# Message passing, last layer, steps 2 to 4: gathered rows go through PSUM before VectorE multiplies them

## The reference, cut to what matters

```
w = _kernel_net(edge_attr, ...).reshape(-1, 16, 16)      # one 16x16 matrix per edge
for i in range(DEPTH):                                   # DEPTH = 4
    msg = einsum('ei,eio->eo', nodes[src], w)            # gather a row, multiply by its edge's matrix
    agg = segment_sum(msg, dst, num_segments=n) * inv_deg
    nodes = gelu(agg + nodes @ root_W[i] + root_b[i])
```

## Time and profile before

| | us |
|---|---|
| median of 3 runs without the profiler | 26865.84 |
| lowest and highest of them | 26846.94, 26884.09 |
| span of the profiled execution, first to last instruction | 31834.1 |

### The profile page before, as it was taken

How to read it: one execution, slowest core, us unless ns; L and a number is a source line. 1 busy time by engine, 2 the same in 40 slices (tenths; PEclk the granted TensorE clock), 3 DMA queues, 4 the chain that set the end, 5 groups by cost and what they waited for, 6 DMA issues and landing times. The chain is left out here.

```text
span 31834.1 us, 357740 instructions
## 1 busy us (share of the span) xinstructions
PE 21003.5 (66%) x95045; PEld 10976.5 (34%) x95045; DVE 19470.8 (61%) x31805; ACT 12595.6 (40%) x14673; POOL 20017.5 (63%) x18077
## 2 busy tenths in 40 slices
PE   4666649999867777756666666566655656465654
PEld 2333326666533333323333333222222222222222
DVE  4444448888756666645555555566665766566665
ACT  4555511111134444431111111455555655455554
POOL 4666657777734444445555555677776777766666
PEclk8777769999877777777777777777777777777777
DMA  1111125555412222212222222444444544444443
GB/s 38 34 33 34 34 59 93 92 92 93 89 42 50 50 49 49 49 44 86 84 86 84 85 84 82 120 138 146 143 127 130 147 140 145 113 136 136 140 135 106
DMA packets 2202951, 2877.61 MB, mean 90 GB/s; under 512 B 962293, under 2 KB 1687075, under 8 KB 2175143
## 3 DMA queue, kind: packets, MB, share of 16 engines
q1 hardware_dynamic: 1369250, 2680.20, 26.7%
q0 software_dynamic: 804512, 169.87, 8.0%
q10 hardware_dynamic: 29088, 26.49, 0.2%
HBM read 2203.20 MB, written 671.60 MB: 90 GB/s over the span
## 5 line engine op out<-in xcount | busy, mean ns | idle before, releaser
L575 POOL DMA_INDIRECT got<-table,idx x15352 | 16035.5, 1045 | 10224.3 <-issue 4522.0
L777 PE MATMUL in_place<-place_hot,tparts 128*128 128x512 bf16 x37600 | 10862.7, 441 | 5734.9 <-issue 2698.7
L777 PEld LDWEIGHTS in_place<-place_hot,tparts 128*128 128x128 bf16 x37600 | 4005.5, 111 | 11806.1 <-issue 7382.3
L940 ACT ACTIVATE near<-place_b,far_lanes 128x512 bf16<-128x512 f16 x9180 | 5713.3, 707 | 61.9 <-DMA place_b<-place_row 61.4
L1078 DVE TENSOR_REDUCE msg<-prod 128x64 f32<-128x1024 f32 x4040 | 4904.5, 1214 | 103.3
L945 ACT ACTIVATE place_hot<-near,one 128x4608 bf16<-128x4608 bf16 x1020 | 4218.3, 4136 | 1004.0 <-remote 810.9
L930 ACT ACTIVATE outb<-run 128x256 f32<-128x256 f32 (+1 forms) x1010 | 739.3, 732 | 8309.1 <-DVEq L1115 6614.4
L1492 POOL DMA_INDIRECT added<-rows,add_idx x2020 | 3318.9, 1643 | 962.2 <-issue 866.7
L1070 DVE TENSOR_TENSOR prod<-w_in,got 128x1024 f32<-128x1024 f32 x2424 | 2909.9, 1220 | 303.7 <-DMA got<-table,idx 176.5
L1535 PE MATMUL acc<-hot,spread 128*128 128x392 bf16 x14544 | 2849.5, 353 | 0.0
L1063 DVE TENSOR_TENSOR wcopy<-wmat,b 128x1024 f32<-128x1024 f32 x808 | 988.3, 1223 | 2445.7 <-remote 2050.1
(11 more groups left out here) (253 smaller groups left out, 18740.6 us busy)
## 6 DMA issues: line engine op xcount, KB each, us to landing
w_in<-kept SPq DMA_DIRECT2D x2424, 512.0 KB
kept<-wcopy SPq DMA_DIRECT2D x808, 512.0 KB
got<-table,idx POOLq DMA_INDIRECT x15352
attr<-in_edge_attr SPq DMA_DIRECT2D x202, 1024.0 KB
place_b<-place_row SPq DMA_DIRECT2D x1020, 128.0 KB
range_b<-range_row SPq DMA_DIRECT2D x1015, 128.0 KB
sums<-outb SPq DMA_DIRECT2D x1010, 128.0 KB
rows<-in_src_row SPq DMA_DIRECT2D x202, 640.0 KB
```

The source lines that it names most:

```text
L575: pool.indirect_dma_start(out=dst[:, j * width:(j + 1) * width], out_offset=None, in_=table, in_offset=bass.IndirectOffsetOnAxis(ap=idx[:, ...
L777: mm = pe.matmul(in_place[b][:, h, :], tparts[:, s, t, :], place_hot[:, b, t, h * XC:(h + 1) * XC], start=(t == 0 and s == 0), stop=(t == ...
L940: act.activation(near[:, t, :], place_b[:, b, :], ACT.Abs, bias=SB["far_lanes"][:, t:t + 1]).then_inc(S["near_made"], 1)
```

## The change

In kind "kernel_kept" alone:

- ScalarE gets a step `rows_over(k)`: it waits for chunk k's 12 gathers, for VectorE to be done with chunk k-2 (`rows_read`), and copies the 12 places' rows (192 float32 per partition) from `got` in SBUF into `rows_p[k % 2]`, one PSUM bank each. It stands between `hot_rows` and `turn_out`, one chunk ahead.
- VectorE waits for that copy (`rows_made`) instead of the gathers. Its first three products read the rows from `rows_p`; the fourth reads TensorE's rows straight from `in_row`. The copy L1019 is gone. `fetched` is raised at the end of the chunk instead of before the last product, together with `rows_read`. `got_used` is not raised any more.
- GpSimd reuses a ring buffer once ScalarE has copied from it.

For the other kinds only the way ScalarE's loop is written out changes (four chunks to a loop instead of two, in the same order).

```
+            rows_p = [ps(f"rows_p{k}", [P, 512])[:, 0:J0 * W] for k in range(HALVES)]
...
+                        if kind == "kernel_kept":
+                            pool.wait_ge(S["rows_made"], k - RING + 1)
+                        else:
+                            pool.wait_ge(got_used[r], q)
...
+                def rows_over(k, b, r, q, first):
+                    act.wait_ge(got_in[r], (q + 1) * (16 * J0))
+                    if not first:
+                        act.wait_ge(S["rows_read"], k - 1)
+                    act.activation(rows_p[b], got[:, r, 0:J0 * W], ACT.Copy).then_inc(S["rows_made"], 1)
...
+                def chunk(k, r, q, at):
+                    i, b = q * (RING // HALVES) + r // HALVES, r % HALVES
+                    if at is None or at + 1 < CHUNKS:
+                        spread_mask(k + 1, 1 - b, at == 0)
+                    hot_rows(k + 2, b, i + 1)
+                    if kind == "kernel_kept" and (at is None or at + 1 < CHUNKS):
+                        rows_over(k + 1, 1 - b, (r + 1) % RING, q + (r + 1) // RING, at == 0)
+                    turn_out(k, b, i, at is not None and at < HALVES)
...
-                        dve.wait_ge(got_in[r], (q + 1) * (16 * J0))
+                        if kind == "kernel_kept":
+                            dve.wait_ge(S["rows_made"], k + 1)
+                        else:
+                            dve.wait_ge(got_in[r], (q + 1) * (16 * J0))
...
+                                if g < GROUPS - 1:
+                                    rows_g = rows_p[b].rearrange("p (j f) -> p j f", f=W)[:, g * G:(g + 1) * G, :]
+                                else:
+                                    dve.wait_ge(S["in_row_made"], k + 1)
+                                    rows_g = in_row[b].rearrange("p (j f) -> p j f", f=FW)
...
-                                bcast(rows_v[:, g * G:(g + 1) * G, 0:D], 2, D), ALU.mult).then_inc(w_used, 1)
+                                bcast(rows_g, 2, D), ALU.mult).then_inc(w_used, 1)
...
-                            if X and g == GROUPS - -(-X // G):
+                            if kind == "relational" and g == GROUPS - -(-X // G):
                                 fetch(k, b, r, c)
...
+                        if kind == "kernel_kept":
+                            dve.sem_inc(S["rows_read"], 1)
+                            dve.sem_inc(S["fetched"], 1)
```

More of the change, by code:

```diff
@@ L650, in edge_pass @@
                  "place_in0", "place_in1", "range_in0", "range_in1", "hot_by_act", "hot_by_dve", "in_place_made", "picked_made", "in_row_made", "fetched",
-                 "kept0", "kept1", "kept2", "kept3", "mask_made", "scanned", "cleared", "w_copied", "near_made", "whole_clear", "whole_in", "whole_step", "parts_made",
+                 "kept0", "kept1", "kept2", "kept3", "mask_made", "scanned", "cleared", "w_copied", "near_made", "rows_made", "rows_read", "whole_clear", "whole_in", "whole_step", "parts_made",
                  "w_in0", "w_in1", "w_in2", "w_in3", "w_in4", "w_in5", "w_in6", "w_in7"]
@@ L757, in chunk @@
                     if at is None or at >= RING:
-                        pool.wait_ge(got_used[r], q)
+                        if kind == "kernel_kept":
+                            pool.wait_ge(S["rows_made"], k - RING + 1)
+                        else:
+                            pool.wait_ge(got_used[r], q)
                     pool.wait_ge(idx_in[r], (q + 1) * 16)
@@ L949, in _ @@
                 spread_mask(0, 0, True)
[L950 to L963, removed]
+                if kind == "kernel_kept":
+                    rows_over(0, 0, 0, 0, True)
+                rounds(act, chunk)
                 if kind == "weighted":
@@ L1066, in product @@
                                 w = wcopy[:, g, :]
+                                rows_g = rows_v[:, g * G:(g + 1) * G, 0:D]
                             else:
@@ L1097, in chunk @@
                         c.step(dve.tensor_tensor(msg[:, b, D:2 * D, :], msg[:, b, 0:D, :], bcast(emix[:, :], 1, D), ALU.mult))
-                    if kind in ("kernel_net", "kernel_kept"):
+                    if kind == "kernel_net":
                         dve.sem_inc(got_used[r], 1)
@@ L1124, in chunk @@
                     assert c.n == per_chunk, c.n
-                per_chunk = {"weighted": 4, "relational": 11, "kernel_net": 7, "kernel_kept": 7}[kind]
+                per_chunk = {"weighted": 4, "relational": 11, "kernel_net": 7, "kernel_kept": 6}[kind]
                 def split_table():
```

## The result

The changed kernel takes 25775.43 us (median of 4 runs, 25755.62 to 25800.32) against 26871.5 us for the kernel before beside it (4 runs, 26846.94 to 26884.09): a ratio of 0.9594 [0.9582, 0.9605], 1096 us less. The forecast was 26,190 us. The time lies inside the predicted range (25,600 to 26,680) but outside the range of case A (25,850 to 26,400), between A and C.

The account below looks back on a forecast made before the run. kernel_kept was taken as barely gather-bound before (14.2 us per chunk) and VectorE-bound after (13.1): 1.1 us times 606 chunks, 670 us off the median, gives about 26,190 us. Range, 8 times in 10: 25,600 to 26,680 us.

Parts of the forecast that it names:

- case A: The forecast: kernel_kept barely gather-bound before, VectorE-bound after; 26,190 us, own range 25,850 to 26,400; chance 0.5.
- case C: kernel_kept gathers cost without the profiler what the trace shows: 17.41 us per chunk before, 1370 us less, 25,500; chance 0.1.
- GpSimd is no longer disturbed: kernel_kept gathers beside VectorE's products take 0.94 instead of 1.96 us; disturbance per chunk falls from 2.46 to 0.2 us.
- So a gather must be cheaper without the profiler.: Gathers in kernel_kept cost 0.98 us each unprofiled instead of 1.245, putting the chunk before at 14.2 us.
- the 4968 us: Gap between the profiled execution of the kernel before, 31834.1 us, and its median without the profiler, 26865.84 us.
- The budget: Splits the 4968 us: kernel_net 2279, kernel_kept the other 2689, or 570 less if other gathers get cheaper.
- D: Rival: VectorE reads repeated rows from PSUM at a lower rate; at 0.5 us more per product, 27,400 us; chance 0.09.
- over on arrival: ScalarE's new wait for the gathers in kernel_kept is already met when it gets there, if gathers lead.
- No new idle time until ACT rows_p: Sign in the kernel_kept profile: VectorE does not newly wait for ScalarE's copied rows, a copy of 0.4 us.
- E: Rival: gain eaten, as late `fetched` ties TensorE's sums to VectorE, or the swap does nothing; 26,870 us; chance 0.07.
- B: Rival: GpSimd is not the bound before, or not relieved; only removing copy L1019 counts, 26,640 us; chance 0.24.
- The forecast of 31,430 us for the profiled execution: Changed kernel under the profiler: TensorE's standstills let GpSimd catch up, so only 230 and at most 176 us are won.

## Why the prediction was right and wrong

**Right: the step on GpSimd, and the direction.** The step "GpSimd is no longer disturbed" held as it was written: gathers beside products at 0.94 to 0.95 us instead of 1.96, mean 960 ns (under the 1000 named). What remains, put at 0.2 us, is 15.12 - 14.95 = 0.17. The prediction laid it to the one-hot work alone (L1004, L1014 in the changed kernel). In the trace that is about a third of it, 0.06 us per chunk; the other 0.10 us is the scan, which has two operands in SBUF as well. Changed kernel, VectorE and then GpSimd:

```profile
17127.04 0.69 DVE L1134 TENSOR_TENSOR_SCAN run<-mask,msg 128x256 f32<-128x256 f32 x1
```

```profile
17127.29 1.19 POOL L575 DMA_INDIRECT got<-table,idx  x1 [0.30 <-issue]
```

The gather that starts inside the scan ends 0.75 us after it.

The rule of the Trainium skill that spoke against it ("SBUF — State Buffer", section Who interferes with whom) infers that descriptor generation goes on beside a tensor_tensor with two SBUF inputs; the runs go against that inference, with 1103 ns against 960, and 671 us between rows in SBUF and rows in PSUM (26446.92 against 25775.43, from two jobs whose times of before differ by 77 us; 699 us against the 25747.98 of the run with the copy put back, in the same job). The other half of that rule, as the prediction tells it, is that such a product holds up a GpSimd instruction that reads SBUF, and a gather does read its indices from `idx` in SBUF: "by that rule nothing is won" did not follow from it. Which access of a gather has to wait no run separates.

**Wrong: what bounds the kernel, through "So a gather must be cheaper without the profiler."** The prediction had the kept passes barely bound by gathers before and bound by VectorE after, at 13.09 us. They are bound by gathers on both sides, at 16.82 and 15.12 us, and the prediction's own sign of being wrong came up: VectorE waits for `rows_p` in 590 of 606 chunks. This is the step that failed. The prediction took TensorE's standstills as something the profiler brings in, and distributed the 4968 us over the stages. What could not be covered it put on the gathers: c = 0.98 us instead of the 1.245 that each row showed.

The budget also shared the 4968 us between kernel_net and kernel_kept, but for 570 us that it allowed to other gathers. The chunks of the two profiles show that weighted and relational passes hold 2330 us of the difference (the relational chunks of the first profile, 24.64 us on average and 15.97 at the least, already said so), and kernel_kept 870 us and not 2689: a kept chunk is 1.43 us shorter without it, not 4.44, and no cheaper gather is needed. The 4968 us were, by all that the runs show, another chip's. Where the timed runs were made a gather costs 0.944 + 0.303 us in a profile whose span is that of the runs without one, so the budget compared two different things. The sum of the cheap gather gave 14.2 us before; it was 16.82.

**The term that was mis-sized.** 12 x 1.245 + 2.46 = 17.41 was case C's chunk before. The 17.41 was one chunk, and the hold-up of a chunk depends on its phase: the mean is 16.82 - 14.95 = 1.87 us. C with the mean gives (1.87 - 0.17) x 606 = 1030 us of the measured 1096. C's mechanism decided, and C had a chance of 0.1 because the budget spoke against it.

**Luck.** That the time fell into the stated range is luck. The forecast was 670 us less, and 1096 came. The gather price was 0.27 us too low, which took 3.2 us from each chunk before and hid that gathers stay the bound after; the hold-up was 0.6 us too high per chunk. The time missed the range of case A, case C's figure of 25,500 lies outside the stated range, and the measured 25775.43 lies between them.

**Step by step.** The copy L1019, put at 0.38 us, is worth nothing in a gather-bound chunk, as the run with the copy put back shows. The products, put at 0, cost 1219 and 1222 against 1226 ns: D falls, and so does the 0.26 us per chunk from the Trainium skill, "Perfetto Trace Analysis", section Optimizing Scalar/DVE Operations, of which these durations show nothing. `rows_over` at 0.4 us measured 0.33 and is hidden in time, but not "over on arrival": the rows say 602 waits. "No new idle time until ACT rows_p" was wrong for the same reason, since VectorE waits in 590 of 606 chunks; it merely waits there instead of for `got` (1120.8 us in place of 1929.5). `fetched`, 3.9 us later in VectorE's order, costs nothing, as put: quarter 0 is released by `place_hot` (593 times), not by VectorE, as the whole period is 2 us longer than forecast. In the run with ten gathers VectorE does release it. Scan to scan 13.1 us came true only there. "No stretch with VectorE waiting for gathers at a period above 15.3 us" did not hold either: behind the gathers, half of the chunks take over 15.5 us. E falls. B falls too: the copy and the fourth product alone give 164 us.

The forecast of 31,430 us for the profiled execution (25798.5) was wrong with its premise. Whether the kernel would take about that on the slow chip was not tried.

## What to carry to other kernels

Put a profile's span beside the unprofiled median first. If they differ by 18%, as 31834 and 26866 do, take the profile again (here the second agreed with the timed runs to 0.1%), and do not spread the difference over the engines, least of all over some of the stages; the prices of single instructions had been right (0.94 and 0.30 us), only the budget was not. A queue that waits for nothing but itself is the bound even at 76 to 78% busy (GpSimd in the kept passes), because its gaps count: multiply instructions by duration plus gap. Where a long row of gathers shares the time with VectorE's products, as here, an operand in PSUM, or only another order, gives their hold-up back; after that each gather moved to an engine with slack is worth its 1.26 us per chunk (771 us for one in 606 chunks) until the next engine is reached, and that must be tried on more than one chip.

## What the hardware did that was not expected

The same kernel took 32184.25 us on one chip and 26758 to 26830 us on three others (26871.5 in the result's job, whose chip is not on record), with a mean granted clock of 0.776 to 0.780 in the seven runs there against 0.853 to 0.855. That is one job on one such chip; whether it is the chip or the hour was not tried. That the first profile came from such a chip is inferred from its time, its clock (0.781) and its chunks in each kind of pass. The clock is lower above all outside the kept passes (0.79 against 0.97 in the relational pass of the two profiles). It does not explain the long kept chunks by itself: they have matmuls 1 to 2.2 us apart with no wait. What keeps them apart is open.

In these traces a product with two SBUF operands holds up only gathers that start well inside it. In kernel_net of the kernel before, products have both operands in SBUF and gathers still average 960 ns. VectorE's timeline, then GpSimd's:

```profile
13005.70 1.22 DVE L1070 TENSOR_TENSOR prod<-wcopy,got 128x1024 f32<-128x1024 f32 x1
```

```profile
13005.67 0.94 POOL L575 DMA_INDIRECT got<-table,idx  x1 [0.30 <-issue]
```

The gather starts 0.03 us ahead of the product, and the next at 13006.92, when the product has just ended. The alternation of copy and product there has about the period of a gather. Counted over that stretch (11820 to 15880 us), 463 gathers start during a product, 374 of them in its last 0.3 us, at 0.95 to 1.01 us on average; the 36 that start 0.05 to 0.15 us after it began take 1.97 us. The `wcopy` instructions (L1063) beside them read one operand from PSUM, and the 757 gathers that start during one take 0.944 us wherever they start. So it is the place in time that keeps kernel_net's mean low; what holds the gathers to that place was not tested.
